# One attention block on one core: projections in fp16 parts, rings of three PSUM banks, a new order on TensorE and a new beginning

## The reference

```python
q, k, v = (proj(w_q), proj(w_k), proj(w_v))            # of layernorm(x), fp32
scores = einsum('bhqd,bhkd->bhqk', q, k) / sqrt(16.)
attn = softmax(scores, axis=-1)
out = einsum('bhqk,bhkd->bhqd', attn, v)
x = x + out.reshape(B, S, 512) @ w_o.T
xq = int4_quant(layernorm(x))                          # scale by the row's mean of |x|
gate, up = bitlinear(xq, w_gate), bitlinear(xq, w_up)  # weights rounded to -1, 0, 1
x = x + bitlinear(int8_quant(up * relu(gate)**2), w_down)
```

## Time and profile before

| | before |
|---|---|
| median of 3 runs | 1143.07 us (1142.91 to 1144.18) |
| profiled execution | 1141.39 us |
| its span, first to last instruction | 1139.6 us |
| mean granted TensorE clock | 0.983 |
| TensorE busy | 1051.8 us, 92% |
| VectorE busy | 884.5 us, 78% |
| ScalarE busy | 738.2 us, 65% |
| GpSimd busy | 143.3 us, 13% |

### The profile page before, as it was taken

The page is one execution under the profiler, slowest core; times in us unless marked ns, Lnnn a source line. Parts: engine busy times, 40 slices in busy tenths (PEclk is TensorE's granted clock), DMA queues, the critical chain, the costliest instruction groups (busy, mean ns, idle before and its releaser), DMA issues.

```text
span 1139.6 us, 18560 instructions
## 1 busy us (share of the span) xinstructions
PE 1051.8 (92%) x6882; PEld 354.3 (31%) x6882; DVE 884.5 (78%) x1573; ACT 738.2 (65%) x885; POOL 143.3 (13%) x282
## 2 busy tenths in 40 slices
PE   4889999999999999999999999999998669888886
PEld 2333222222222222222222222222222235444543
DVE  3265588988988897898888889889997267788874
ACT  4631277766777776776677677667778536656664
POOL 2200011011101201201110110111000021111210
PEclk9889999999999999999999999999999979999998
DMA  9430013102202300230220121022253251111110
GB/s 349 153 86 1 1 31 78 33 20 66 58 18 66 66 11 20 66 65 10 76 57 13 35 73 41 20 66 57 96 154 85 62 152 37 39 37 37 37 46 28
DMA packets 43862, 69.63 MB, mean 61 GB/s; under 512 B 3334, under 2 KB 21766, under 8 KB 43526
## 3 DMA queue, kind: packets, MB, share of 16 engines
q1 hardware_dynamic: 43782, 68.56, 21.6%
HBM read 46.99 MB, written 21.23 MB: 60 GB/s over the span
## 4 chain that ended last, share of the span: by engine, by line
PE 64%; DVE 12%; ACT 5%; issue 5%; DMA 5%; POOL 2%; SPq 1%; DVEq 0%; POOLq 0%; ACTq 0%
PE ps L360 20%; PE ps L312 17%; PE ps L297 10%; PE ps L341 8%; PE ps L275 4%; DVE mx L765 3%; PE ps L421 2%; ACT PB L571 2%; DMA QK<-parts_d 2%; DVE hm L860 2%; POOL rstd L1027 1%; DMA parts_d<-spl 1%; PE ps L443 1%; DVE bst L808 1%; DVE PB L806 1%
## 5 line engine op out<-in xcount | busy, mean ns | idle before, releaser
L765 DVE TENSOR_REDUCE mx<-ps 128x1 f32<-128x512 f32 x1024 | 653.3, 685 | 122.6 <-PE ps L312 116.8
L571 ACT ACTIVATE PB<-ps 128x1024 f32<-128x1024 f32 x512 | 522.5, 1024 | 196.5 <-PE ps L341 191.2
L312 PE MATMUL ps<-QK 48*128 48x512 f16 x1024 | 354.6, 385 | 11.4 <-DVE mx L765 8.2
L360 PE MATMUL ps<-PB,Vg 128*32 128x256 f32 (+1 forms) x3192 | 303.2, 451 | 8.7 <-ACT PB L571 4.6
L341 PE MATMUL ps<-QK 50*128 50x512 f16 x1024 | 300.4, 382 | 1.2 <-DMA QK<-nmT 1.1
L312 PEld LDWEIGHTS ps<-QK 48*128 48x128 f16 x1024 | 92.4, 92 | 431.3 <-DVE mx L765 379.6
L297 PE MATMUL ps<-XV,wqk 128*128 128x512 f32 x256 | 144.4, 656 | 0.0
L360 PEld LDWEIGHTS ps<-PB,Vg 128*32 128x32 f32 x3192 | 63.5, 107 | 110.9 <-issue 97.6
L421 PE MATMUL ps<-tu,Vg 128*128 128x344 bf16 x256 | 49.1, 315 | 24.6 <-DVE XV L849 24.6
L275 PE MATMUL ps<-wv,XV 128*128 128x512 f32 x128 | 69.4, 649 | 0.0
L399 PE MATMUL ps<-wo,XV 128*128 128x512 f32 x128 | 61.1, 622 | 6.0 <-DVE PB L806 5.2
(11 more groups left out here) (117 smaller groups left out, 657.7 us busy)
## 6 DMA issues: line engine op xcount, KB each, us to landing
parts_d<-spl SPq DMA_DIRECT2D x64, 128.0 KB
QK<-parts_d SPq DMA_DIRECT2D x32, 256.0 KB, 5.1
att_d<-OS SPq DMA_DIRECT2D x32, 256.0 KB
PB<-x SPq DMA_DIRECT2D x28, 256.0 KB, 2.9
QK<-parts_d SPq DMA_DIRECT2D x32, 128.0 KB, 4.7
XV<-att_d SPq DMA_DIRECT2D x2, 2048.0 KB, 8.4
QK<-rden_d SPq DMA_DIRECT2D x8, 512.0 KB, 7.8
out<-PB SPq DMA_DIRECT2D x16, 256.0 KB, 2.0
```

Of the source, the lines that this page charges most:

```text
L312: nc.tensor.matmul(ps[:, 4 + at % 2, :], QK[rows, sup % 2, 2 * set_ + p, 0, half * HALF + qt * P:half * HALF + (qt + 1) * P], QK[rows, sup ...
L360: last = nc.tensor.matmul(ps[32 * h:32 * h + 32, 6, part * n:part * n + n], Vg[:, set_, kt, h, :], PB[:, step % 2, h, part * n:part * n + ...
L571: nc.scalar.activation(PB[:, step % 2, 2 * pair:2 * pair + 2, :], ps[:, 2 * pair:2 * pair + 2, :], ACT.Exp, scale=exp_reg).then_inc(probs, 1)
L765: nc.vector.tensor_reduce(mx[:, unit % 2, qt * 4 + head, kh:kh + 1], ps[:, 4 + at % 2, :], AX.X, ALU.max)\
```

## The change

The new kernel computes the same, in another order and with other operands:

- The projections of q, k and v take x (times 1024) and the weights (times a power of two) as fp16 high and low parts and add three products, high by high, high by low and low by high: 12 fp16 matmuls where there were 4 fp32 ones. All weights of q and k are split once in the beginning and stay in SBUF, so the loads per superunit are gone. VectorE computes the low parts.
- Jobs run six units ahead of their use, k before q, two matmuls in each of steps 2 to 7 of a unit. Every unit but the last six has one.
- Score items have a ring of three banks (0 to 2), transposed scores one of three banks (3 to 5) with one exponential of 128x512 each, PB has three buffers, and banks 6 and 7 alternate between the value sums of one unit, and the jobs and the transposed maxima of the next.
- A step on TensorE is item, T, item, T, job matmuls, item, T, item, T, and last the value sum of the step before, never cut. The first two T are those of side 0, the last two those of side 1.
- The maxima's transposes come in step 1 of the unit before, and ScalarE copies them out in step 2.
- AHEAD is 16 instead of 11, and RAMP_TILE 2 instead of 5: 64 items are done before the first step.
- The beginning has a new order on every engine; POOL rounds the gate weights, VectorE the up weights between maxima. The tail's code is the same but for where one tile lies.

```diff
-RAMP_TILE = 5
-AHEAD = 11
+RAMP_TILE = 2
+AHEAD = 16
...
+JOBS_AHEAD = 6
+S_BANKS, T_BANK, T_BANKS, AV_BANK = 3, 3, 3, 6
...
+        PRODUCTS = ((0, 0), (0, 1), (1, 0))
...
+            for m, (a, b) in enumerate(PRODUCTS):
+                last = nc.tensor.matmul(ps[:, 4 + t % 2, :], xparts[t // BT][:, a, k, t % BT * P:(t % BT + 1) * P],
+                                        wv[:, b, k, :], start=(k == 0 and m == 0), stop=(k == KT - 1 and m == 2))
...
+            if at < S_BANKS:
+                pe.wait_ge(xt_copy, BT)
+                pe.wait_ge(xl_ready, BT)
+            else:
+                pe.wait_ge(s_used, at - S_BANKS + 1)
...
+            side, p = i // 2, i % 2
+            n = sup * 4 * STEPS + 4 * step + i
...
+            if n >= T_BANKS:
+                pe.wait_ge(probs, n - T_BANKS + 1)
...
-                jobs = not last and step < 16
+                at, r = sup * 4 + step // KEYT, step % KEYT
                 item(step, 0)
                 pe_scoresT(pe, sup, step, 0)
                 item(step, 1)
+                pe_scoresT(pe, sup, step, 1)
+                if job_in(at) and r >= 2:
+                    for m in range(2 * r - 4, 2 * r - 2):
+                        pe_job(pe, job_in(at), m)
+                item(step, 2)
+                pe_scoresT(pe, sup, step, 2)
+                item(step, 3)
+                pe_scoresT(pe, sup, step, 3)
                 if step > 0:
-                    pe_av(pe, sup, step - 1, 0, 1 if jobs else 2)
-                item(step, 2)
-                pe_scoresT(pe, sup, step, 1)
-                item(step, 3)
-                if jobs:
-                    pe_job(pe, sup + 1, region, step // 4, step % 4)
-                elif step > 0:
-                    pe_av(pe, sup, step - 1, 1, 2)
...
+                    pe_av(pe, sup, step - 1)
+                elif sup > 0:
+                    pe_av(pe, sup - 1, STEPS - 1)
+                if r == 1 and at + 1 < UNITS:
+                    pe_max_rows(pe, at + 1)
...
                 for k in range(KT):
                     pe_tile_values(pe, t, k)
-                    if t >= RAMP_TILE and item < 4 * AHEAD:
-                        pe_scores(pe, 0, item // 32, item % 32)
-                        item += 1
+                    if t >= RAMP_TILE and k % 2 == 1:
+                        item = items(2)
                         if item == 40:
-                            pe_max_rows(pe, 0, 0)
+                            pe_max_rows(pe, 0)
...
             if t == BT:
-                act.wait_ge(w_min, 8)
+                act.wait_ge(w_tern[0], 4)
+                act.wait_ge(w_tern[1], 4)
...
-            nc.scalar.activation(PB[:, step % 2, 2 * pair:2 * pair + 2, :], ps[:, 2 * pair:2 * pair + 2, :],
+            nc.scalar.activation(PB[:, at % 3, 2 * (i % 2) + i // 2, :], ps[:, T_BANK + n % T_BANKS, :],
                                  ACT.Exp, scale=exp_reg).then_inc(probs, 1)
...
             for step in range(STEPS):
+                at, r = sup * 4 + step // KEYT, step % KEYT
+                if r == 2 and at + 1 < UNITS:
+                    act_rows(act, at + 1)
                 act_exp(act, sup, step, 0)
                 act_exp(act, sup, step, 1)
-                if step % KEYT == 0 and step > 0:
-                    act_sums(act, sup, step // KEYT - 1)
-                if not last and step < 16 and step % 4 == 3:
-                    act_job(act, sup + 1, step // 4)
+                if r == 0 and job_in(at - 1):
+                    act_job(act, job_in(at - 1))
+                if r == 1 and at > 0:
+                    act_sums(act, at - 1)
+                act_exp(act, sup, step, 2)
+                act_exp(act, sup, step, 3)
...
-            for t in range(BT):
+            for t in range(4):
                 act_tile_copy(act, t)
             act_squares(act, 0)
             act_squares(act, 1)
+            act_weights(act, 1, 0, 256)
+            act_tile_copy(act, 4)
+            act_tile_copy(act, 5)
+            act_weights(act, 0, 0, 256)
+            act_tile_copy(act, 6)
+            act_tile_copy(act, 7)
+            act_squares(act, 2)
+            act_job(act, 0)
+            act_abs(act, 0, GATE_ORDER[0])
+            act_job(act, 1)
+            act_abs(act, 0, GATE_ORDER[1])
+            act_weights(act, 2, 0, HID)
...
             for k in range(4 * AHEAD):
...
+                if k == 1:
+                    dve_total(dve, 1)
+                    dve_factor(dve, 1)
...
+                if 9 <= k < 13:
+                    dve_ternary(dve, 1, k - 9, k - 9)
+                if k == 16:
+                    dve_weights(dve, 0, 256, 256, 5)
+                if k == 19:
+                    for t in range(8, 12):
+                        dve_tile_rest(dve, t)
+                        dve_normalise(dve, t + 4)
+                if k == 27:
+                    for t in range(12, 16):
+                        dve_tile_rest(dve, t)
```

More of the change, by code:

```diff
@@ L218, in first @@
             return isinstance(n, int) and n < limit
-        def item_at(sup, unit, k):
-            rest = 33 * unit + k - (1 if k < 8 and not (first(sup, 1) and unit == 0) else 0)
-            return rest
-        def rows_at(sup, unit):
-            return 33 * unit + (40 if not (isinstance(sup, int) and sup == SUPERS - 1 and unit == 3) else 32)
         def step_items(step):
@@ L335, in pe_scoresT @@
                     pe.wait_ge(aux_in, 128)
-            if sup > 0 or step > 0:
-                pe.wait_ge(probs, sup * (2 * STEPS) + (2 * step + p - 1))
-            for side in range(2):
-                rows = slice(side * SIDE, side * SIDE + AUG)
-                last = nc.tensor.matmul(ps[:, 2 * p + side, :],
-                                        QK[rows, sup % 2, 2 * set_ + p, 1, kt * P:(kt + 1) * P],
-                                        QK[rows, sup % 2, 2 * set_ + p, 0, half * HALF:(half + 1) * HALF],
-                                        start=True, stop=True)
@@ L345, in pe_scoresT @@
-            last.then_inc(st_psum, 1)
-        def pe_av(pe, sup, step, part, parts):
-            unit, kt = step // KEYT, step % KEYT
-            set_ = unit // 2
-            n = HALF // parts
-            if part == 0:
-                pe.wait_ge(probs, sup * (2 * STEPS) + (2 * step + 2))
-            if kt == 0 and part == 0:
+                    pe.wait_ge(v_copy, TILES)
+                    pe.wait_ge(w_fac, 2)
+            if n >= T_BANKS:
+                pe.wait_ge(probs, n - T_BANKS + 1)
@@ new lines, in pe_scoresT, with pe_av @@
+            rows = slice(side * SIDE, side * SIDE + AUG)
+            nc.tensor.matmul(ps[:, T_BANK + n % T_BANKS, :],
+                             QK[rows, sup % 2, 2 * set_ + p, 1, kt * P:(kt + 1) * P],
+                             QK[rows, sup % 2, 2 * set_ + p, 0, half * HALF:(half + 1) * HALF],
+                             start=True, stop=True).then_inc(st_psum, 1)
+        def pe_av(pe, sup, step):
+            unit, kt = step // KEYT, step % KEYT
+            set_, at = unit // 2, sup * 4 + unit
+            pe.wait_ge(probs, sup * 4 * STEPS + (4 * step + 4))
+            if kt == 0:
@@ L356, in pe_av @@
                 if unit % 2 == 0:
                     pe.wait_ge(vg_ready, sup * 2 + (set_ + 1))
-                pe.wait_ge(os_copy, sup * 4 + (unit + 1))
-            for h in range(GH):
-                last = nc.tensor.matmul(ps[32 * h:32 * h + 32, 6, part * n:part * n + n], Vg[:, set_, kt, h, :],
-                                        PB[:, step % 2, h, part * n:part * n + n],
-                                        start=(kt == 0 and part == 0), stop=(kt == KEYT - 1 and part == parts - 1))
@@ L363, in pe_av @@
-            if part == parts - 1:
-                last.then_inc(av_done, 1)
-        def pe_superunit(pe, sup, region, last):
+                if job_in(at - 1):
+                    pe.wait_ge(job_copy, job_in(at - 1) + 1)
+                if at > 0:
+                    pe.wait_ge(rows_used, at + 1)
+                if at == UNITS - 1:
+                    pe.wait_ge(w_fac, 3)
+            for h in range(GH):
+                last = nc.tensor.matmul(ps[32 * h:32 * h + 32, av_bank(at), :], Vg[:, set_, kt, h, :],
+                                        PB[:, (sup * STEPS + step) % 3, h, :], start=(kt == 0), stop=(kt == KEYT - 1))
@@ L368, in item, with pe_superunit @@
+            last.then_inc(av_done, 1)
+        def pe_superunit(pe, sup, last):
             def item(step, j):
@@ L547, in act_abs, with wsum_first @@
+        def wsum_first(w, q):
+            return q == (GATE_ORDER[0] if w == 0 else 0)
         def act_abs(act, w, q):
-            if q == 0:
-                act.wait_ge(raw_in[w], 16 * (1, 1, 5)[w])
+            if w == 1 and q == 0:
+                act.wait_ge(w_low, 4)
+            if wsum_first(w, q):
+                act.wait_ge(raw_in[w], 16 * (4, 1, 5)[w])
                 if w == 2:
@@ L759, in dve_max @@
             qt, p, side, kh = item_of(k)
```

(12 more changed lines are left out.)

705 lines of the change are left out of this document (402 added, 303 removed).

## The result

The changed kernel takes 1162.79 us in the median of 4 runs (1160.01 to 1168.88); beside it the kernel before took 1142.99 (1137.16 to 1144.18). The ratio is 1.0191, with a 95% interval of 1.0137 to 1.0245. I had predicted 1107, with a range up to 1125: the direction was wrong. (Medians here are over all executions; the ratios leave out two that took longer than the others of their kernel, 1884.33 us of e2 and 1157.76 us of the kernel before.) The profiled execution took 1163.81 us with a span of 1161.9, which is 58.0 more than the 1103.9 of my sum.

The account below looks back on a forecast made before the run. TensorE was taken to bound steps with a job, the maxima's banks those without. Span 1139.6 - 27.0 (attention steps) - 8.7 (earlier first exponential) = 1103.9, median 1107.4; range 1092 to 1125.

Parts of the forecast that it names:

- The steps: Attention steps: 3.03 us with a projection job, 2.48 without; a unit of 8 steps with a job 23.5.
- The fp16 job's price: Projection jobs on TensorE: 0.216 us per fp16 matmul, two a step, plus 0.09 for each change of array layout.
- the bank rings: Steps without a job: waits for banks freed by maxima and exponentials, then the value sum, give 2.48 us.
- my 3 us for the reciprocal and its passes: Units 28 and 29: reciprocal of the sums and two ScalarE passes add 3 us, 43.3 in all.
- Rival D: Steps keep their 3.0 us average, bound by ScalarE's four starts or the T bank ring; median 1134; chance 4%.
- Rival C: Same-side successors on TensorE pay their weight loads: 0.37 us per step with a job, 58 us, median 1165; chance 7%.
- GpSimd's price: Beginning: GpSimd rounds the gate weights in 8 passes of 1.7 us, 13 us in all.
- the cover: Beginning: GpSimd's gate passes hide beside the up weights, else tiles 8 to 11 are late by what is left.
- The rest of the beginning: Before the attention: ScalarE leads, values wait until 75 and end near 84, first exponential at 129 against 137.7 us.
- rival B: Long beginning: the new chain through all engines eats its gain, first exponential at 142, median 1120; chance 18%.
- the last 16 steps: Steps without scores: nothing hides the wait of the fourth transposed score, 2.38 us each, 40.4 in all, a loss of 3.4.
- the 240.9 behind them: Everything after the last 16 steps: 240.9 us, with the tail unchanged.

Follow-up runs that it names:

- e2: Changed kernel with unread score matmuls in the 64 empty places of the last 16 steps: 1145.74 us, ratio 1.0019 to the kernel before.
- e5: Kernel e1 with five GpSimd passes of 128x1376 added at its end to price them: 1.34 us with multiply and add, 4.85 us with the other operations.
- e1: Changed kernel with the gate weights rounded on VectorE again instead of GpSimd: 1136.90 us, ratio 0.9915 to the kernel before.
- e9: Changed kernel with GpSimd's eight gate passes written as multiply and add, without clipping, so another output: 1137.62 us, ratio 0.9963 to the kernel before.
- e6: Changed kernel with the edits of e1 and e2 together: 1119.79 us, ratio 0.9821 to the kernel before.
- e7: Kernel e6 with GpSimd computing the inverse deviation of tiles 8 to 11 ahead of its last part-making job: 1119.98 us, ratio 0.9823 to the kernel before.
- e10: Kernel e6 with two unread scores instead of four in each of the last 16 steps: 1121.22 us in a single run.

## Why the prediction was wrong, point by point

**The steps: right in their length.** Steps with a job 3.04 for 3.03, the plain ones 2.49 for 2.48, units 23.48 for 23.5. The fp16 job's price (0.216, and 0.09 for each change of layout) and the bank rings held. The fourth score's start was wrong (1.30 for 1.50), without effect. Units 0 to 29 are 4.5 over in 30 units: 1.7 in unit 0, which begins at a granted clock of 0.53 (164 to 171 us) and whose second step took 4.63, and 2.0 in units 28 and 29, where my 3 us for the reciprocal and its passes were too few: one step took 5.96, with a wait of 2.03 for a maximum and a granted clock of 0.50 behind it (843.6 to 847). In e2 the clock stayed up there, and the same step took 4.52. Rival D is out.

**Rival C is out, though its time came true.** It said 1165 and the result is 1163, but its mechanism isn't there: T2 to T3 and S1 to T1 on one side start 0.22 apart (480.01 to 480.23 above, and the x2 row at 481.30 ends where 0.22 puts its second start), and all of C's 58 us would have stood in the steps with a job. The rule of the Trainium skill that a weight load overlaps only matmuls of other row groups (page "TensorE: Matmul & The Clock Gate", section "Part 3: Packing small matmuls — row/col tiling") finds no support in these rows. A time that agrees is no evidence for a mechanism; the rows named for it are.

**The failed step is GpSimd's price.** I wrote "POOL now rounds the gate weights: 8 passes at 0.62 x 1376 / 512 = 1.7 are 13 us; they hide beside the up weights". The row taken was the nearest by engine and shape, but of another operation (a copy written as multiply by 1 and add 0). A pass took 4.85, eight took 40, and that is 21.8 us at the first exponential. The price should have had an upper end. The Trainium skill, page "GPSIMD Engine Reference", section "4.1 Engine selection", calls one-input elementwise work on GpSimd roughly line-rate. e5 agrees with that for multiply and add (1.34) and not for the two pairs of operations that the kernel uses (4.85, where VectorE took 0.87 and 0.52 in e1).

**The second failed step is the cover.** "They hide beside the up weights" holds for no length: VectorE's normalisations wait for a pass each, and with them the maxima queued behind and TensorE. e9 puts 3.5 us on it at passes of 1.34; at 4.85 it is the way by which most of the length reaches TensorE, whose wait grew from 6.45 to 23.64. So the two steps failed together, and 21.8 + 3.5 divides them only in the sense of those runs. I had named who waits if the passes are long, "else tiles 8 to 11 are late by what is left", but not that the passes hold VectorE itself.

**The rest of the beginning was 10 us short.** e1 has 139.6 for 129, and this was lost before 94 us: from the transposes of tiles 8 to 11 on (94.33 in e6) until the exponential at 139.1 it is 44.8 us where I had 84 to 129, 45. In e6 TensorE waits 6.54 for the maximum behind the normalisations, works at a granted clock of 0.50 from 72 to 78 (six matmuls, half a value tile, in 2.72 and 2.27 instead of 1.47), and waits 0.69, 1.55 and 0.21 for maxima queued among VectorE's passes over the up weights. I had counted 3 us for a spell at low clock and no such waits. The path was wrong too: I had ScalarE lead and the values wait for it until 75. In e6 the first values start at 55.49, the only wait for ScalarE among them is 2.14 (until 62.97), and what holds TensorE until 73.03 is VectorE's queue behind GpSimd's deviation. So the values began earlier than I had them and lost more than that in the waits; 10.6 is what was left. (The terms that I added up to 60 there make 62.) What each is worth alone was not tried; e7 shows that taking one away need not pay. My rival B (142) was about this, and e1 lies nearer to it than to the forecast.

**The third failed step is the last 16 steps.** I had the wait, 1.07 + 1.31 = 2.38 (2.39 measured at full clock, 2.40 in e2), and wrote that nothing hides the wait there. I put the clock at nothing there and didn't ask what a wait in every step does to it, though I had put low clock into the beginning. The term cost 18.9 us, at a granted clock of 0.52 and 3.69 a step; e2 gives back all but 0.6. The comparison with the kernel before was off as well: the stretch 861.70 to 898.70 of the earlier trace rows has 31 exponentials, not 32, since it ends where the last step's first one starts. It is 15 steps, so the loss of 3.4 that I forecast was 1.3, and the last step of the kernel before (2.08) was counted again in the 240.9 behind them. The forecast should have been 2.1 us lower, so the miss is larger by that, and what lies behind the steps is about 0.8 over and not 1.3 under.

**Sum.** 21.8 (length of the passes) + 3.5 (turns) + 10.6 (the rest of the beginning, before 94 us) + 18.9 (last steps) + 4.5 (units 0 to 29) - 1.3 = 58.0. The range was too narrow since the unknown operation on GpSimd had one price and no bounds, and the clock of the last steps had no term.

## What to carry to other kernels

Moving an elementwise pass to an idle engine needs the price of that very operation there, not of the nearest shape, and the question whether the engine it leaves has work that must take turns with it. Where a change empties part of TensorE's steps, count them at both levels of the clock; unread matmuls in the empty places were worth 17 us here, and two of four did as well in the one run that tried it. Test a rival by its rows, not by its time: here the wrong one was 2 us off.

## What the runs showed of the hardware that I had not expected

- A tensor-scalar pass of 128x1376 on GpSimd takes 1.34 us with multiply and add and 4.85 with subtract and minimum, subtract and add, or maximum and multiply, fp32 or bf16, alone or in company (subtract and add was run in company only).
- Four normalisations on VectorE, 1.92 us together in e1, took 20.18, 13.16 and 6.13 us beside GpSimd's passes, each time the length of four passes within 0.3.
- Steps with 0.47 us of idle time in 2.39, and one or two with 1.35 to 1.39, were followed by a granted clock of 0.50 for the rest of the stage, at 3.69 a step; with 0.26 in 2.40, and two with 1.13 and 1.16 (e10), it stayed at 1.00. More matmuls made the stage 18 us shorter.
- A score started 0.22 us before a transposed score that stands ahead of it in the program, on the other side of the array (kernel after, 481.08 and 481.30).
- A lead of 1.5 us of TensorE at 88 us was gone 10 us later, when the granted clock was 0.66 against 1.00 in the same stretch (e7, e6).
